# Three of sixteen low halves from GpSimd to VectorE, and the gates' copy at the head of its chunk

## The chip, the core and the metric

One core of a Trainium2 chip runs the whole program. It has TensorE (matmuls into PSUM), VectorE, ScalarE, GpSimd (which works on SBUF here) and the DMA queues; each runs its own instruction stream, and they wait for one another on semaphores. The metric is device time in microseconds, lower is better. Of the kernel before, three runs took 857.78, 859.27 and 860.64 us; the median is 859.27.

## The reference

4096 tokens of 128 features go through two blocks with residuals.

```python
x = x + gnn(layernorm(x), adj, ...)       # two-head masked attention over 4096 tokens
# then the block that the change touches; xf = layernorm(x), 4096 x 128:
gate_scores = xf @ Wg + bg                # 8 experts
mask = one_hot(top_k(gate_scores, 2)).sum(-2)
h = gelu(einsum('td,edh->teh', xf, W1) + b1)    # all 8 experts, 256 hidden
y = einsum('teh,ehd->ted', h, W2) + b2
out = x + einsum('ted,te->td', y, mask)   # the two chosen experts, weight 1 each
```

## The kernel before

The attention takes the first three quarters of the time, tile by tile of 128 rows. The change touches only the feed-forward block behind it, which runs from about 657 us to the end.

The tokens stand in 8 chunks j of 512 (`NC`, `CH`). Each chunk computes all 8 experts e densely, and a 0/1 gate per token and expert picks two of them at the end. The precision of float32 comes from pairs of float16: a value is kept as a high half (rounded to f16) and a low half (the rest), and each product is three matmuls: high by high, high by low, low by high.

For an expert the hidden layer comes in two blocks b of 128 (`HB` is 2), so a chunk has 16 hidden blocks of 128x512, numbered 2e+b. The path of one is:

- TensorE, `up` (L986 to L988): three 128x512 matmuls into one of 4 PSUM banks. It waits for the Gelu that empties the bank.
- ScalarE, `ffn` (L468): Gelu from PSUM to `hid`, f32. Then (L471) a copy to `hid_hi`, f16.
- GpSimd, `ffn` (L337): `hid - hid_hi` to `hid_lo`, f16, all of them in the order of 2e+b. `hid`, `hid_hi` and `hid_lo` lie in the buffer `prob`, so the profile calls all three that. They have 8 slots, four experts.
- TensorE, `down` (L1006 to L1008): 24 matmuls of 128x128 into a PSUM bank of two, for both blocks of e. It waits for both low halves (`hid_lo_ready`, L995) and for the combination of expert e-2 (`combined`), which empties the bank.
- VectorE, `combine` (L772): four 128x128 operations, `x_sb = psum * gate + x_sb`.

TensorE's order is written out in `ffn`: in step e it does up(e), then down(e-2), the latter two steps of the next chunk for e of 6 and 7. So down(j, 0) runs in step 2 of the chunk, and the last two of a chunk in steps 0 and 1 of the next.

Beside the experts runs the second bias, which depends on the gate. VectorE copies the gates of the chunk, 128x32, to f16 (`halve_gates`, L753). TensorE transposes them in step 3, between up(3) and down(1) (`gate_transpose`, L965, four operations). ScalarE copies the result (L458), TensorE multiplies it with the bias in step 4 (L974, L975), and VectorE adds that to `x_sb` behind the combination of e=2 (`add_b2`, L760).

VectorE's order in a chunk is: combine 0, halve_gates, combine 1, combine 2, add_b2, combine 3 to 7. In the first chunk (`early`) it also finishes the last two tiles of the attention: normalise (L654) behind combine 0, and behind combine 5 the ranking of the last four tiles' gates (`rank_gates`, L680 to L687, seven of them at L687, 128x4 each) and behind combine 6 their choice (`choose_gates`, L693 to L695). All these read and write SBUF. Every engine does its stream strictly in the written order.

Of the kernel before, what the change touches and what calls it, by code (L numbers as in the profile page):

```python
# [9 lines left out]
ALU = mybir.AluOpType  # L10
# [15 lines left out]
E, H, HB = 8, 256, 2  # L26
# [21 lines left out]
UP_BANKS = 4  # L48
HID_RING = 8
DOWN_LAG = 2  # L50


def build(nc, x, adj, wq, wk, wv, wr, wd, bias, wg, bg, w1, b1, w2, b2, out):
# [6 lines left out]
    with ExitStack() as ctx:  # L60
# [3 lines left out]
        def sem(name):  # L64
            return ctx.enter_context(nc.semaphore(name))
# [58 lines left out]
        hid = prob[:, 1, :].rearrange("p (r c) -> p r c", r=HID_RING)  # L124
        hid_hi = area(0, 0, NC // 2).bitcast(F16).rearrange("p (r c) -> p r c", r=HID_RING)
        hid_lo = area(0, NC // 2, NC // 2).bitcast(F16).rearrange("p (r c) -> p r c", r=HID_RING)
# [69 lines left out]
        hid_raw_ready = sem("hid_raw_ready")  # L196
        hid_hi_ready = sem("hid_hi_ready")
        hid_lo_ready = sem("hid_lo_ready")
        down_done = sem("down_done")
        combined = sem("combined")  # L200

# [10 lines left out]
        def copies_by_dve(j, units):  # L212

            return NU // 2 * j + units // 2

        block = ctx.enter_context(nc.Block())
        N_QKV_W, N_W = 3, 8
# [49 lines left out]
        @block.gpsimd  # L267
        def _(pool):
            pool.memset(ident[:, :], 0.0).then_inc(ident_zero, 1)
            pool.wait_ge(ident_zero, 1)  # L270
            pool.affine_select(out=ident[:, :], in_=ident[:, :], compare_op=ALU.not_equal, fill=1.0, base=0,
                               pattern=[[-1, P]], channel_multiplier=1).then_inc(ident_ready, 1)
            pool.memset(wrd[:, :, :, :], 0.0).then_inc(wrd_zero, 1)
            pool.memset(expo[:, :], -0.5).then_inc(ones_ready, 1)

            def load_adj(i, par):

                for c in range(2):
                    if not isinstance(i, int) or i >= 2:
                        pool.wait_ge(masked, NU * i - 12 + 4 * c)  # L280
                    cols = slice(c * HALF, (c + 1) * HALF)
                    pool.dma_start(mask[:, par, cols], adj[bass.ds(i * P, P), cols],  # L282
                                   max_dma_last_dim=8192).then_inc(adj_in[par][c], 16)

            def inverse_std_x(i):

                part = slice(i * X_TILES, (i + 1) * X_TILES)
                pool.wait_ge(var_ready, i + 1)
                pool.tensor_tensor(rstd[:, part], ve[:, part], expo[:, part], ALU.pow).then_inc(rstd_ready, 1)

            def split_weights(n, raw, pair):

                pool.tensor_scalar(raw, raw, W_UP, 0.0, ALU.mult, ALU.add).then_inc(w_split_chain, 1)
                pool.wait_ge(w_split_chain, 3 * n + 1)
                pool.tensor_scalar(pair[:, 0, :], raw, 1.0, 0.0, ALU.mult, ALU.add).then_inc(w_split_chain, 1)
                pool.wait_ge(w_split_chain, 3 * n + 2)
                pool.tensor_tensor(pair[:, 1, :], raw, pair[:, 0, :], ALU.subtract).then_inc(w_split_chain, 1)

            pool.wait_ge(ones_ready, 1)
            for i in range(X_PARTS):  # L300
                inverse_std_x(i)
            load_adj(0, 0)
            load_adj(1, 1)
            pool.wait_ge(k_lo_ready, NC)
            pool.wait_ge(w1_in, 16)
            split_weights(0, w1_raw, w1_pair)
            pool.wait_ge(w2_in, 16)
            split_weights(1, w2_raw, w2_pair)
            pool.wait_ge(w_in, 16 * N_W)
            split_weights(2, wg_sb[:, :], wg_pair)  # L310
            split_weights(3, b2_sb[:, :], b2_pair)
            pool.tensor_scalar(ident16[:, :], ident[:, :], 1.0, 0.0, ALU.mult, ALU.add).then_inc(w_split_chain, 1)

            def inverse_std(t0):

                pool.wait_ge(ve2_ready, t0 + PAIR)
                pool.tensor_tensor(rstd2[:, :], ve2[:, :], expo[:, 0:PAIR], ALU.pow).then_inc(rstd2_ready, PAIR)

            def load_behind_post(i, par):

                if par == 0:
                    inverse_std(i - 6)
                load_adj(i, par)

            for i in range(2, 6):
                load_adj(i, i % 2)
            pairs(pool, 6, NT, load_behind_post)
            for t0 in range(NT - 6, NT, PAIR):
                inverse_std(t0)

            def ffn(j, par):
                for e in range(E):
                    for b in range(HB):

                        slot = (2 * e + b) % HID_RING
                        pool.wait_ge(hid_hi_ready, 16 * j + 2 * e + b + 1)  # L336
                        pool.tensor_tensor(hid_lo[:, slot, :], hid[:, slot, :], hid_hi[:, slot, :],  # L337
                                           ALU.subtract).then_inc(hid_lo_ready, 1)

            pairs(pool, 0, NC, ffn)  # L340
# [141 lines left out]
        def _(dve):  # L482
# [265 lines left out]
            def halve_gates(j):  # L748

                if not isinstance(j, int) or j > 0:  # L750
                    dve.wait_ge(gatet_psum, j)
                settled()
                dve.tensor_copy(gate16, gate[:, bass.ds(j * TPC, TPC), :]).then_inc(gate16_ready, 1)  # L753

            def add_b2(j):
# [4 lines left out]
                dve.tensor_tensor(x_sb[:, rows, :], ps[:, PREP0, :].rearrange("p (t d) -> p t d", d=D), x_sb[:, rows, :],  # L760
                                  ALU.add).then_inc(acc_ready, 1)

            def combine(j, e):

                dve.wait_ge(down_done, 8 * j + e + 1)
                if e == 3:
                    dve.wait_ge(acc_ready, j + 1)
                elif e > 0:
                    dve.wait_ge(combined, 8 * j + e)
                for t in range(TPC):  # L770
                    row = x_sb[:, bass.ds(j * TPC + t, 1), :].rearrange("p t d -> p (t d)")
                    ins = dve.scalar_tensor_tensor(row, ps[:, DOWN0 + e % 2, t * D:(t + 1) * D],  # L772
                                                   gate[:, bass.ds(j * TPC + t, 1), e:e + 1].rearrange("p t e -> p (t e)"),
                                                   row, ALU.mult, ALU.add)
                ins.then_inc(combined, 1)

            def ffn(j, par, early=False):

                for e in range(E):
                    combine(j, e)  # L780
                    if e == 0:
                        halve_gates(j)
                    if e == 2:
                        add_b2(j)
                    if early and e == 0:
                        normalise(NT - PAIR)
                    if early and e == 3:
                        x2t_low(NT - PAIR, bank=PREP0 + 1)
                    if early and e == 5:
                        keep_logits(NT - PAIR, bank=PREP0 + 1)  # L790
                        rank_gates(1, RANKED_EARLY, NT)
                    if early and e == 6:
                        choose_gates(1, RANKED_EARLY, NT)
# [6 lines left out]
        def _(pe):  # L800
# [189 lines left out]

            def down(j, e, early=False):

                pe.wait_ge(hid_lo_ready, 16 * j + 2 * e + 2)
                if not (early and e < 2):
                    pe.wait_ge(combined, 8 * j + e - 1)  # L995
                elif e == 0:
                    pe.wait_ge(sat_ready, NT)
                else:
                    pe.wait_ge(logit_ready, NT - PAIR)
                for t in range(TPC):  # L1000
                    bank = ps[:, DOWN0 + e % 2, t * D:(t + 1) * D]
                    for b in range(HB):
                        slot = (2 * e + b) % HID_RING
                        rows = slice(t * P, (t + 1) * P)
                        cols = slice((HB * e + b) * D, (HB * e + b + 1) * D)
                        pe.matmul(bank, hid_hi[:, slot, rows], w2_pair[:, 0, cols], start=(b == 0), stop=False)  # L1006
                        pe.matmul(bank, hid_hi[:, slot, rows], w2_pair[:, 1, cols], start=False, stop=False)  # L1007
                        ins = pe.matmul(bank, hid_lo[:, slot, rows], w2_pair[:, 0, cols], start=False, stop=(b == HB - 1))  # L1008
                ins.then_inc(down_done, 1)

            def ffn(j, par, early=False):

                for e in range(E):
# [9 lines left out]
                    if e == 4:  # L1023
                        gates_b2(j)
                    if e >= DOWN_LAG:
                        down(j, e - DOWN_LAG, early)
                    elif not early:
                        down(j - 1, e + E - DOWN_LAG)

# [26 lines left out]
```

## Time and profile before

| | |
|---|---|
| runs shown, median | 859.27 us (857.78 to 860.64) |
| the profiled execution's own time | 858.09 us |
| its span | 856.1 us |
| TensorE matmuls busy | 812.1 us, 95% |
| TensorE weight loads | 596.3 us, 70% |
| ScalarE | 678.9 us, 79% |
| VectorE | 624.6 us, 73% |
| GpSimd | 221.3 us, 26% |

The profile page gives for each engine the busy time, and for each group of instructions the count, the mean duration and the idle time ahead of them with what ended it. Matmuls overlap: a 128x512 one shows 0.38 us but the next starts earlier, so distances between starts tell the rate, not durations. GpSimd's share of 26% is an average; in the feed-forward block its busy tenths are 7 or 8, those of TensorE 9, of VectorE 3 or 4. TensorE's granted clock is full (1.00, which is 2.4 GHz) in that block but for a stretch of some 6 us near its start at half of it, behind a pause of TensorE.

### The profile page before, as it was taken

The numbers are of one execution on the slowest core, as the hardware profiler recorded it, in microseconds if no ns is written. First come the engines' busy times: TensorE is split into PE (matmuls) and PEld (weight loads), VectorE is DVE, ScalarE is ACT, GpSimd is POOL, SyncE is SP. The second block draws the span as 40 slices with busy tenths as digits, with TensorE's granted clock in tenths as the row PEclk, the third lists the DMA queues.
The fourth block names the chain that finished last, engine by engine and source line by source line (L and its number), as shares of the span: only waits on it lengthen the run. The fifth ranks groups of instructions, "written<-read, shape, count | busy, mean of one in ns | idle before, by whom it ended". The sixth has DMA issues, their size and how long they took to land.

```text
span 856.1 us, 31746 instructions
## 1 busy us (share of the span) xinstructions
PE 812.1 (95%) x12080; PEld 596.3 (70%) x12080; DVE 624.6 (73%) x1506; ACT 678.9 (79%) x1099; POOL 221.3 (26%) x233
## 2 busy tenths in 40 slices
PE   4969999999999999999999999999987889999997
PEld 1627777777777777777777777777765656666675
DVE  6587888888888888888888888888883374444444
ACT  3838887878788787887878788787877678998985
POOL 4180000100100000010000001000000778878785
PEclk9989999999999999999999999999999899999999
DMA  8515533443343344334334433433100000000000
GB/s 219 108 22 91 82 58 58 66 75 55 58 77 55 55 70 71 55 60 75 55 55 74 67 55 62 73 55 57 29 0 2 2 14 14 14 13 12 12 12 12
DMA packets 40900, 44.96 MB, mean 53 GB/s; under 512 B 22168, under 2 KB 32160, under 8 KB 40864
## 3 DMA queue, kind: packets, MB, share of 16 engines
q0 software_dynamic: 9216, 33.56, 24.7%
q1 hardware_dynamic: 31216, 10.71, 5.4%
q8 instruction: 24, 0.39, 0.2%
q10 hardware_dynamic: 432, 0.20, 0.1%
q14 instruction: 12, 0.10, 0.0%
HBM read 71.72 MB, written 2.10 MB: 86 GB/s over the span
## 4 chain that ended last, share of the span: by engine, by line
PE 72%; POOL 17%; issue 6%; DVE 3%; DMA 1%; POOLq 1%; DVEq 0%; ACT 0%
PE ps L892 28%; PE ps L861 19%; PE ps L876 19%; POOL prob L337 17%; PE ps L903 2%; DVE prob L577 1%; PE ps L817 1%; PE ps L822 1%; PE ps L830 1%; PE ps L911 1%; PE ps L808 1%; DMA x_sb<-in_x 1%; POOLq L336 0%; DVE stats L501 0%; DVE mask L545 0%
## 5 line engine op out<-in xcount | busy, mean ns | idle before, releaser
L577 DVE CUSTOM_DVE_ANT_0 prob<-ps,mask 128x1024 f32<-128x1024 f32 x256 | 312.0, 1220 | 90.4 <-PE ps L861 84.6
L406 ACT ACTIVATE prob<-prob,nmax 128x1024 f32<-128x1024 f32 x256 | 292.8, 1144 | 9.9 <-DVE nmax L585 9.9
L892 PE MATMUL ps<-pt,v_sb 128*64 128x128 f32 x4096 | 251.6, 276 | 0.0
L892 PEld LDWEIGHTS ps<-pt,v_sb 128*64 128x64 f32 x4096 | 221.0, 137 | 13.4 <-issue 7.5
L421 ACT ACTIVATE pt<-ps 128x1024 f32<-128x1024 f32 x128 | 131.1, 1024 | 112.6 <-PE ps L876 112.6
L876 PEld LDWEIGHTS ps<-ident,prob 64*128 64x128 f32 x4096 | 151.9, 139 | 79.4 <-issue 79.3
L861 PE MATMUL ps<-k_half,q_row 64*128 64x512 f16 x1536 | 190.0, 380 | 4.8 <-DVE low L577 4.8
L876 PE MATMUL ps<-ident,prob 64*128 64x64 f32 x4096 | 182.9, 228 | 10.3 <-DVE pt L595 5.7
L337 POOL TENSOR_TENSOR prob<-prob 128x512 f16<-128x512 f32 x128 | 148.2, 1160 | 38.5 <-ACT prob L471 33.6
L282 POOL DMA_DIRECT2D mask<-in_adj x64 | 35.5, 554 | 429.4 <-DVE low L577 429.4
L772 DVE SCALAR_TENSOR_TENSOR x_sb<-ps,k_half,x_sb 128x128 f32 (+1 forms) x256 | 72.1, 344 | 99.5 <-PE ps L1008 99.2
L861 PEld LDWEIGHTS ps<-k_half,q_row 64*128 64x128 f16 x1536 | 71.5, 96 | 68.4 <-issue 9.6
L468 ACT ACTIVATE prob<-ps,b_sb 128x512 f32<-128x512 f32 x128 | 86.9, 679 | 25.4 <-PE ps L988 23.6
L1006 PE MATMUL ps<-w_pair,prob 128*128 128x128 f16 x512 | 90.3, 221 | 6.6 <-POOL prob L337 4.7
L595 DVE COPY pt<-ps 128x512 f32<-128x512 f32 x128 | 88.1, 688 | 9.7 <-PE ps L876 8.7
L1008 PE MATMUL ps<-w_pair,prob 128*128 128x128 f16 x512 | 90.1, 220 | 0.0
L1007 PE MATMUL ps<-w_pair,prob 128*128 128x128 f16 x512 | 90.1, 220 | 0.0
L471 ACT ACTIVATE prob<-prob 128x512 f16<-128x512 f32 x128 | 80.7, 630 | 4.1
L418 ACT ACTIVATE pt<-ps 128x512 f32<-128x512 f32 x128 | 75.1, 587 | 1.1 <-PE ps L876 1.1
L1006 PEld LDWEIGHTS ps<-w_pair,prob 128*128 128x128 f16 x512 | 50.4, 98 | 14.6 <-POOL prob L337 5.4
L1007 PEld LDWEIGHTS ps<-w_pair,prob 128*128 128x128 f16 x512 | 50.5, 99 | 5.1
L1008 PEld LDWEIGHTS ps<-w_pair,prob 128*128 128x128 f16 x512 | 50.5, 99 | 0.0
(96 smaller groups left out, 657.7 us busy)
## 6 DMA issues: line engine op xcount, KB each, us to landing
mask<-in_adj POOLq DMA_DIRECT2D x64, 512.0 KB, 5.6
q_row<-q_nat SPq DMA_DIRECT2D x128, 32.0 KB, 4.8
x_sb<-in_x SPq DMA_DIRECT2D x4, 512.0 KB, 7.0
out<-x_sb SPq DMA_DIRECT2D x8, 256.0 KB, 2.3
pt<-in_L_ffn_W SPq DMA_DIRECT2D x1, 1024.0 KB, 6.5
wq_sb<-in_L_gnn_Wq ACTq DMA_DIRECT2D x1, 64.0 KB, 2.9
wk_sb<-in_L_gnn_Wk ACTq DMA_DIRECT2D x1, 64.0 KB, 4.5
wv_sb<-in_L_gnn_Wv ACTq DMA_DIRECT2D x1, 64.0 KB, 5.6
```

The costliest lines, as they stand in the source:

```text
L337: pool.tensor_tensor(hid_lo[:, slot, :], hid[:, slot, :], hid_hi[:, slot, :], ALU.subtract).then_inc(hid_lo_ready, 1)
L406: act.activation(prob[:, h, cols], prob[:, h, cols], ACT.Exp, bias=nmax[:, h:h + 1], scale=-1.0, accum_out=sums[:, j, h, p:p + 1]).then_in ...
L421: act.activation(pt[:, u, :, :].rearrange("p k (b q) -> p b k q", b=2), ps[:, TR0:TR0 + 2, :].rearrange("p b (k q) -> p b k q", k=KT), ACT ...
L468: act.activation(hid[:, slot, :], ps[:, (2 * e + b) % UP_BANKS, :], ACT.Gelu, bias=b1_sb[:, e, b:b + 1], scale=1.0 / W_UP).then_inc(hid_ra ...
L577: dve.tensor_tensor_reduce(out=prob[:, h, col_of(p)], in0=ps[:, 2 * (u % 2):2 * (u % 2) + 2, :].rearrange("p b c -> p (b c)"), in1=mask[:, ...
L595: dve.tensor_copy(pt[:, u, :, DH:P], ps[:, TR0 + 1, :].rearrange("p (k q) -> p k q", k=KT)).then_inc(pt_by_dve, 1)
L861: ins = pe.matmul(ps[:, 2 * (u % 2) + half, :], q_row[part, par, h, a, :], k_half[part, h, b, cols], start=first, stop=final)
L876: ins = pe.transpose(ps[:, TR0 + half, t * DH:(t + 1) * DH], prob[part, h, (p * KT + t) * P:(p * KT + t + 1) * P], ident[part, part])
L892: ins = pe.matmul(ps[dims, AV, 0:P], v_sb[:, tile, dims], pt[:, UNITS.index((h, p)), t, :], start=(tile == 0), stop=(tile == NT - 1))
L1006: pe.matmul(bank, hid_hi[:, slot, rows], w2_pair[:, 0, cols], start=(b == 0), stop=False)
L1007: pe.matmul(bank, hid_hi[:, slot, rows], w2_pair[:, 1, cols], start=False, stop=False)
L1008: ins = pe.matmul(bank, hid_lo[:, slot, rows], w2_pair[:, 0, cols], start=False, stop=(b == HB - 1))
```

## The change

A constant names three experts, e = 2, 4 and 6. Their second hidden block (b = 1) gets its low half from VectorE (`low_hidden`), not from GpSimd; that is three of the sixteen of a chunk, 24 in all. GpSimd's loop leaves it out. VectorE does the one of expert e+1 just ahead of the combination of e, so behind the combination of e-1, and for e+1 = 4 behind `add_b2` as well. It counts on a semaphore of its own, and `down` waits for both counts. The gates' copy moves from behind combine 0 to the head of the chunk, ahead of combine 0.

```diff
+DVE_LOWS = (2, 4, 6)
+        hid_lo_by_dve = sem("hid_lo_by_dve")
+        POOL_LOWS = HB * E - len(DVE_LOWS)
+
+        def lows_by_dve(j, e):
+
+            return len(DVE_LOWS) * j + sum(1 for d in DVE_LOWS if d <= e)
+
+        def lows_by_pool(j, e):
+
+            return POOL_LOWS * j + HB * (e + 1) - sum(1 for d in DVE_LOWS if d <= e)
@@ GpSimd
                 for e in range(E):
-                    for b in range(HB):
+                    for b in range(1 if e in DVE_LOWS else HB):
@@ VectorE
+            def low_hidden(j, e):
+
+                slot = (2 * e + 1) % HID_RING
+                dve.wait_ge(hid_hi_ready, 16 * j + 2 * e + 2)
+                dve.tensor_tensor(hid_lo[:, slot, :], hid[:, slot, :], hid_hi[:, slot, :],
+                                  ALU.subtract).then_inc(hid_lo_by_dve, 1)
@@ VectorE, ffn
+                halve_gates(j)
                 for e in range(E):
+                    if e + 1 in DVE_LOWS:
+                        low_hidden(j, e + 1)
                     combine(j, e)
-                    if e == 0:
-                        halve_gates(j)
                     if e == 2:
                         add_b2(j)
@@ TensorE, down
-                pe.wait_ge(hid_lo_ready, 16 * j + 2 * e + 2)
+                pe.wait_ge(hid_lo_ready, lows_by_pool(j, e))
+                pe.wait_ge(hid_lo_by_dve, lows_by_dve(j, e))
```

## Rows read from the trace of the kernel before

**Rows 1.** Waits of TensorE, last stage: engine, line, releaser: us, times, longest.

```profile
PE ps L965 <- DVE k_half L753: 5.4, 7, 0.9
PE ps L1006 <- POOL prob L337: 4.7, 2, 4.0
PE ps L1006 <- DVE x_sb L772: 1.9, 1, 1.9
```

**Rows 2.** Busy time (instructions) by engine in one stretch, then granted clock, DMA share, GB/s.

```profile
760.00:780.00 20.00, 19.25 (x223) 13.78 (x221) 8.82 (x30) 17.83 (x29) 15.98 (x14) 1.00 0.04 13
```

**Rows 3.** TensorE's timeline in one chunk: start us, us, engine, line, operation [idle before <-releaser].

```profile
765.35 0.38 PE L988 MATMUL ps<-x2t_hi,w_pair 128*128 x1
766.48 0.39 PE L965 MATMUL ps<-ident,k_half 128*8 128x128 f16 x4 [0.75 <-DVE k_half L753]
766.79 0.23 PE L1006 MATMUL ps<-w_pair,prob 128*128 128x128 f16 x1
775.15 0.38 PE L988 MATMUL ps<-x2t_hi,w_pair 128*128 x1
775.36 0.22 PE L1006 MATMUL ps<-w_pair,prob 128*128 128x128 f16 x1
778.00 0.22 PE L1006 MATMUL ps<-w_pair,prob 128*128 128x128 f16 x1
```

**Rows 4.** VectorE's timeline in the same chunk and the start of the next.

```profile
764.71 1.13 DVE L772 SCALAR_TENSOR_TENSOR x_sb<-ps,k_half,x_sb 128x128 f32 x4 [1.64 <-PE ps L1008]
765.75 0.67 DVE L753 CAST k_half<-k_half 128x32 f16 x1
771.74 1.13 DVE L772 SCALAR_TENSOR_TENSOR x_sb<-ps,k_half,x_sb 128x128 f32 x4 [2.16 <-PE ps L1008]
772.97 0.69 DVE L760 TENSOR_TENSOR x_sb<-ps,x_sb 128x512 f32 x1
774.38 1.12 DVE L772 SCALAR_TENSOR_TENSOR x_sb<-ps,k_half,x_sb 128x128 f32 x4 [0.71 <-PE ps L1008]
784.92 1.13 DVE L772 SCALAR_TENSOR_TENSOR x_sb<-ps,k_half,x_sb 128x128 f32 x4 [1.51 <-PE ps L1008]
788.73 0.67 DVE L753 CAST k_half<-k_half 128x32 f16 x1
```

**Rows 5.** Timelines of VectorE and TensorE around the start of the second chunk.

```profile
694.19 1.02 DVE L695 TENSOR_SCALAR k_half<-k_half 128x32 f32<-128x32 f32 x1
695.25 2.16 DVE L772 SCALAR_TENSOR_TENSOR x_sb<-ps,k_half,x_sb 128x128 f32<-128x128 f32 x8
697.33 0.17 DVE L753 CAST k_half<-k_half 128x32 f16<-128x32 f32 x1
697.55 0.39 PE L965 MATMUL ps<-ident,k_half 128*8 128x128 f16 x4 [0.93 <-DVE k_half L753]
```

**Rows 6.** Line L687 in the last stage: operation, count, duration min/median/max ns, starts.

```profile
L687 DVE TENSOR_TENSOR k_half<-k_half x7: 167/987/1145, 687.7 to 691.5; 128x4 f32<-128x4 f32 x7
```

**Rows 7.** ScalarE's timeline behind the gate transposes of that chunk.

```profile
767.62 0.57 ACT L458 ACTIVATE k_half<-ps 8x512 f16<-8x512 f16 x1
769.07 0.69 ACT L468 ACTIVATE prob<-ps,b_sb 128x512 f32<-128x512 f32 x1 [0.89 <-PE ps L988]
```

**Rows 8.** Groups by shape, whole span: out<-in, count, busy us, mean ns, idle before.

```profile
L538 DVE TENSOR_TENSOR k_half<-ps,k_half 128x512 f16<-128x512 f32 x8 | 5.3, 687 | 1.8 <-ACT k_half L374 1.8
L628 DVE SCALAR_TENSOR_TENSOR o_act<-o_pre 128x256 f32<-128x256 f32 x16 | 6.7, 416 | 0.0
L337 POOL TENSOR_TENSOR prob<-prob 128x512 f16<-128x512 f32 x128 | 148.2, 1160 | 38.5 <-ACT prob L471 33.6
```

**Rows 9.** GpSimd's timeline at the sixth expert (e=5) of that chunk.

```profile
773.79 2.40 POOL L337 TENSOR_TENSOR prob<-prob 128x512 f16<-128x512 f32 x2 [0.89 <-ACT prob L471]
```

**Rows 10.** Line L995, a wait ahead of the second layer, on TensorE's queue: durations in ns.

```profile
L995 PEldq ALU_OP  x33: 32/32/32, 712.5 to 845.1; - x33
L995 PEldq EVENT_SEMAPHORE  x20: 51/51/51, 673.2 to 849.8; - x20
```

## The prediction

> **What bounds the kernel now.** I read the waits of TensorE first, over the last stage only, because the change touches nothing ahead of it. Beyond its start, that stage has two kinds of wait [rows 1]: 5.4 us in 7 pieces at L965, the gate transposes, until VectorE's copy of the gates (L753), and 1.9 us once at L1006 until a combination. The 4.7 us until GpSimd are 4.0 us before the very first second-layer matmul and 0.7 us before the last expert's; neither falls at an expert whose low half moves. Then the table by stretches [rows 2]: TensorE is busy 19.25 of 20 us at clock 1.00, GpSimd 15.98, VectorE 8.82. So TensorE sets the pace and GpSimd is nowhere late within a chunk. The chain of waits walks along GpSimd's L337 for 17% of the span, which is misleading: with its pieces stands "issue", and no matmul in the steady part waits for it.
>
> Then TensorE's own timeline in one chunk [rows 3]. In a run of matmuls without a wait a 128x512 one starts 0.216 us after the one before (775.15, then 775.36), although its modelled duration is 0.38. The last one of the first layer's fourth expert (e=3) starts at 765.35, so TensorE could go on at 765.57; the transposes start at 766.48. The loss is 0.91 us, 0.16 more than the 0.75 the row names (0.38 less 0.22, the modelled tail). The expert period without a stall is 778.00 - 775.36 = 2.64 us. VectorE's timeline [rows 4] shows the cause: the combination of e=0 starts at 764.71 and ends at 765.84, the copy follows at 765.75 and takes 0.67 us to 766.42, and 0.06 us later TensorE starts. The same copy takes 0.17 us at 697.33 [rows 5], where GpSimd had nothing to do.
>
> **The change, part by part.**
>
> *The copy moves ahead of all combinations of the chunk.* It now stands right behind the previous chunk's last combination, the one at 784.92, which ends at 786.05. Beside GpSimd the copy takes 0.67 us, and the longest that any such small two-port operation took is 1.145 us (L687, [rows 6]), so it is done by 787.2 at worst. The period is 788.73 - 765.75 = 22.98 us, so the next transposes could start at 765.57 + 22.98 = 788.55: 1.3 us to spare. The semaphore it waits for, the previous chunk's transposes, fired some 19 us earlier. What is late next: TensorE goes straight from up(3) to the transposes and down(1), then up(4), whose first Gelu would be ready at 769.07 - 0.91 = 768.16, while ScalarE's copy of the transposed gates ends at 767.62 + 0.57 = 768.19 [rows 7]: ScalarE is just in time. Over a chunk it is busy 17.83 / 20 x 22.98 = 20.5 us [rows 2], so at a period of 22.1 it is still not the bound. So the whole stall goes. Sum over the stage: 5.4 + 7 x 0.16 = 6.5 us. (In the second chunk the piece is 0.93 + 0.16 = 1.09 us: the transposes at 697.55 could have started at 696.46 [rows 5]. There the copy would follow the combination that starts at 695.25 and ends at 696.3, so it is done at 696.5 even if nothing before it gets shorter; and L695, which took 1.02 us at 694.19 beside GpSimd's second low half of e=2, gets shorter as that one goes.) In the first chunk there is no stall and TensorE waits neither way.
>
> *Three low halves move to VectorE.* GpSimd's takes 1.16 us [rows 8]. Nobody waits for these, so taking 24 of 128 away from GpSimd (28 us of busy time) is worth nothing by itself. On VectorE: 128x512 with f16 out is 0.687 us with one operand in PSUM (L538), and 128x256 with both in SBUF 0.416 us (L628); 256 more elements at VectorE's rate in these two rows make the second about 0.69 us too. Bounds 0.69 alone and 0.69 + 1.15 behind GpSimd's operation; never below 0.69. Do they fit? e=2: behind the combination of e=0, from 765.75 to 766.44; down(2) starts more than an expert period behind down(1) at 766.79 [rows 3], so after 769.4, 3 us to spare. e=6: in the 1.51 us of idle time that a combination in the even run has ahead of it [rows 4]; down(6) comes 5.3 us behind down(4), and it fits alike. e=4 is the tight one: combination of e=2 from 771.74, the second-layer bias at 772.97 to 773.66, then the low half, then the combination of e=3 at 774.38 [rows 4]. Operations without a wait of their own start about 0.09 us before the recorded end of the last (765.75 against 765.84), so 773.57 to 774.26. That is before 774.38, and 1.1 us ahead of down(4) at 775.36. GpSimd's next, the first half of e=5, wants to start at 773.79 [rows 9], 0.22 us behind VectorE. If the two exclude each other GpSimd is held until 774.26, ends its pair at about 776.7, and down(5) is at 778.00. All of these shift together by the 0.91 us, so the order holds afterwards. I take nothing for this part, with the loss of that race as a rival.
>
> The rows show the exclusion: seven operations of 4 elements (L687) took up to 1.145 us where 0.167 is their least, all beside GpSimd's back-to-back low halves. The Trainium skill (SBUF — State Buffer, Who interferes with whom) says that a VectorE operation with two SBUF inputs and a GpSimd operation that reads SBUF exclude each other for a whole instruction, and that the issue order decides who is blocked. That speaks against this change, whose added operations are of that kind. By it the sum stays 5.2 us if VectorE is first and becomes rival A's if GpSimd is; without any exclusion it stays 5.2 us.
>
> *A second semaphore wait ahead of each second-layer group on TensorE.* Its queue handles such a wait in 0.051 us, with 0.032 us for the arithmetic ahead of it [rows 10]: 0.083 us. With the present two waits, down(1) starts 0.31 us after the first of four transposes, 0.08 us more than four steps of 0.056 (an expert period less six of 0.216, through 24). A third would make 0.14 into 0.22 from matmul to matmul. Behind a 128x512 matmul 0.216 us cover that; behind the short ones of the gates (down(1) and down(2) of each chunk) it is exposed. Bounds: 0, and 64 x 0.083 = 5.3 us. I take 16 x 0.083 = 1.3 us, since at 775.15 to 775.36 nothing of the two waits shows.
>
> *Ends.* The chunk order at the very end is the same: e=7 stays with GpSimd. The first 4.0 us stall stays. The first chunk's copy now comes before its first combination, beside the short GpSimd operation that the stall begins with: between 0 and the copy's own 0.17 us [rows 5], and I take 0.
>
> Sum: -6.5 + 1.3 = **-5.2 us**. The profiled execution took 858.09 us (span 856.1 and 2.0 around it), so it would be 852.9; the median of the runs shown is 1.2 us higher, 859.27, and from it comes **854.0**.
>
> **Rivals.**
>
> A. GpSimd wins the race at e=4. VectorE's low half then waits for 773.79 + 1.16 = 774.95, ends at 775.64, and down(4) starts 0.06 us later instead of at 775.36: 0.33 us per chunk, 2.7 us in all; result -2.5 us, 856.7. For: only 0.22 us between the two, worked out from an overlap of another pair. Against: both hang on the same TensorE stretch, so the gap doesn't wander.
>
> B. VectorE is starved of the shared access at e=4: it gets in only behind both halves of e=5, at 776.19, and ends at 776.88. down(4) is 1.58 us late in each chunk, 12.6 us; -5.2 + 12.6 = +7.4, 866.7, slower. It decides from a delay of 0.65 us per chunk, that is when the low half ends behind 775.95. For: GpSimd leaves only 0.08 us between its two. Against: the seven L687, of which none waited longer than one operation.
>
> C. The third wait is exposed at every group: 5.3 us against 6.5, so -1.2, 858.1, no change. For: TensorE's queue must pass two instructions per 0.056 us in the second layer, little reserve. Against: 0.21 us of cover, and rows with no sign of two waits.
>
> D. The transposes are still late, for another releaser (the copy blocked, or ScalarE at e=4 later than I reckon): half of the 6.5 stays, -2.0, 857.3, within the noise.
>
> **How the numbers follow.** Forecast 0.70, A 0.12, C 0.09, D 0.04, B 0.05. What can be told from no change is 0.3%, 2.6 us. A lies on that bound, 0.07 of it count as faster and 0.05 as same. Faster 0.77, same 0.05 + 0.09 + 0.04 = 0.18, slower 0.05. The range: below, the wait costs nothing and the run lies with the profiled one: 859.27 - 6.5 - 1.2 = 851.6. Above, it takes in A and most of D: 857.3. Left out are C and B, 0.14, and a little of the rest.
>
> **What would show it.** Right: no wait at L965 for L753; transposes 0.22 us behind the last matmul of up(3); chunk period about 22.1 to 22.2 us instead of 22.98; L753 right behind the last combination; new VectorE operations of about 0.69 us, the one of e=4 ahead of GpSimd's; clock 1.00 throughout. Wrong: L1006 waiting for VectorE's low half at e=4 (A, B: 0.3 or 1.6 us), gaps ahead of every L1006 with no releaser (C), L965 waiting still (D).

## The result and the profile after

The changed kernel took 851.53 us (median of 4 runs, 851.02 to 852.68); the kernel before took 858.52 beside it (4 runs, 857.45 to 860.64). The ratio is 0.9919, 95% interval 0.9903 to 0.9935, so 7.0 us (5.6 to 8.3) less. I had forecast 854.0, 5.2 us less, in a range from 851.6. The direction and the place were right. The size was not, and the time lies 0.07 us below the range. Two later comparisons of the same kernel, on different chips, gave 0.9929 (0.9911 to 0.9947) and 0.9938 (0.9924 to 0.9952), 6.1 and 5.3 us less. Microseconds beside a ratio are worked out from it, here and below.

The waits of TensorE in the feed-forward block of the kernel after, from the view of waits (the line numbers are new: L1027 is the first matmul of the second layer, L985 the gate transposes):

```profile
PE ps L1027 <- POOL prob L349: 4.7, 2, 4.0
PE ps L1027 <- DVE x_sb L791: 1.9, 1, 1.9
```

Of the three kinds in [rows 1] the one at the transposes is gone; the two others are as they were, to the tenth. The same stretch as in [rows 2] now has TensorE busy in all 20 us, and GpSimd 2.5 us less:

```profile
760.00:780.00 20.00, 20.00 (x234) 14.45 (x232) 10.93 (x33) 18.60 (x30) 13.48 (x12) 1.00 0.05 13
```

TensorE's timeline after, at the place of [rows 3]: the last matmul of up(3), the transposes, down(1).

```profile
762.03 0.38 PE L1008 MATMUL ps<-x2t_hi,w_pair 128*128 x1
762.34 0.39 PE L985 MATMUL ps<-ident,k_half 128*8 128x128 f16 x4
762.66 0.23 PE L1027 MATMUL ps<-w_pair,prob 128*128 128x128 f16 x1
```

From 762.03 to 762.34 it is 0.31 us, where it was 1.13 [rows 3]. That is 0.82 us per chunk, not the 0.91 that I reckoned with. From transposes to down(1) it is 0.32 us with three waits, and was 0.31 with two (starts are printed to 0.01 us; copy_alone below has two waits and 0.32 us).

Parts of VectorE's timeline after, from the last combination of one chunk on (L765 is the gates' copy, L779 the new low halves):

```profile
758.62 1.12 DVE L791 SCALAR_TENSOR_TENSOR x_sb<-ps,k_half,x_sb 128x128 f32 x4 [1.51 <-PE ps L1029]
759.71 0.76 DVE L765 CAST k_half<-k_half 128x32 f16 x1
761.26 1.24 DVE L791 SCALAR_TENSOR_TENSOR x_sb<-ps,k_half,x_sb 128x128 f32 x4 [0.79 <-PE ps L1029]
762.42 0.68 DVE L779 TENSOR_TENSOR prob<-prob 128x512 f16<-128x512 f32 x1
768.84 0.69 DVE L772 TENSOR_TENSOR x_sb<-ps,x_sb 128x512 f32 x1
769.45 0.68 DVE L779 TENSOR_TENSOR prob<-prob 128x512 f16<-128x512 f32 x1
770.24 1.12 DVE L791 SCALAR_TENSOR_TENSOR x_sb<-ps,k_half,x_sb 128x128 f32 x4
```

The copy ends at 760.47, 1.9 us ahead of the transposes. It still takes 0.76 us, since GpSimd is at work beside it, but nobody waits for it there. The low half of e=4 starts at 769.45, 0.08 us before the recorded end of the bias, as forecast. GpSimd's first half of e=5 follows 0.20 us later and is the one that is held:

```profile
769.65 1.50 POOL L349 TENSOR_TENSOR prob<-prob 128x512 f16<-128x512 f32 x1 [2.12 <-ACT prob L483]
```

It takes 1.50 us where 1.16 is usual. All 24 low halves on VectorE took nearly the same time, so in none of the chunks was VectorE the one to wait; this is the line over the whole kernel after, with minimum, median and maximum in ns:

```profile
L779 DVE TENSOR_TENSOR prob<-prob x24: 677/682/689, 670.4 to 840.4; 128x512 f16<-128x512 f32 x24
```

Where the time went, from the starts of single matmuls in TensorE's timelines. "Start" is the first matmul of the feed-forward block, "gates" the first gate transpose of a chunk.

| us | before | after |
|---|---|---|
| start | 656.98 | 657.48 |
| start to gates of the first chunk | 14.63 | 13.57 |
| to gates of the second | 25.94 | 24.82 |
| six further chunks | 137.84 | 132.94 |
| to the end | 20.71 | 20.69 |
| span | 856.1 | 849.5 |

The rows give +0.50, -1.06, -1.12, -4.90 and -0.02, in sum -6.6. The way between gates accounts for 1.12 + 4.90 = 6.0, of which 5.9 are the stall: in the second chunk the transposes came 1.31 us behind the last matmul of up(3), and now come 0.31 us behind it, so 1.00 of the 1.12 is stall (the rest is the end of the half-clock stretch, which before reached past the first gates). What remains are +0.50 in the attention, which the change doesn't touch, and -1.06 ahead of the first gates, where TensorE had no such stall. There the two traces differ in the clock. These are stretches of 1 us (TensorE's busy time and its number of matmuls, then the granted clock, the DMA share and GB/s) of the kernel before:

```profile
665.00:666.00 1.00, 0.05 (x1) 0.55 0.00 0
666.00:667.00 1.00, 1.00 (x11) 0.50 0.06 16
670.00:671.00 1.00, 1.00 (x3) 0.50 0.00 0
671.00:672.00 1.00, 1.00 (x7) 0.54 0.00 0
```

and of the kernel after:

```profile
666.00:667.00 1.00, 0.56 (x9) 0.93 0.00 0
667.00:668.00 1.00, 1.00 (x13) 0.50 0.08 16
670.00:671.00 1.00, 1.00 (x6) 0.86 0.00 0
671.00:672.00 1.00, 1.00 (x18) 1.00 0.00 0
```

In both, TensorE stood idle for 4.0 us before that, and the clock went from 2.4 to 1.2 GHz. Before, it had fallen while TensorE was still idle and was low from 665.1 to 671.9, 6.8 us; after, it fell when TensorE was at work again and was low from 666.9 to 670.3, 3.4 us (a slice of mean clock m was low for 2(1 - m) of its length). These replace the "some 6 us" of the section on the profile before and the 6.3 and 3.6 us of the expectations below.

### The profile page after: what moved, and what is told of

It reads as the page before. It is cut to its first block, busy times and chain, and to the rows that moved or that the text cites. A ratio compares the mean times of both kernels' runs of the same rounds, so it can differ in the third digit from the quotient of the medians.

```text
span 849.5 us, 31821 instructions
## 1 busy us (share of the span) xinstructions
PE 811.7 (96%) x12080; PEld 597.7 (70%) x12080; DVE 639.2 (75%) x1530; ACT 679.0 (80%) x1099; POOL 195.5 (23%) x209
## 4 chain that ended last, share of the span: by engine, by line
PE 73%; POOL 14%; issue 8%; DVE 3%; DMA 1%; ACT 0%; POOLq 0%; DVEq 0%
PE ps L912 28%; PE ps L881 19%; PE ps L896 19%; POOL prob L349 14%; PE ps L923 2%; PE ps L837 1%; PE ps L842 1%; PE ps L850 1%; DVE prob L589 1%; PE ps L931 1%; PE ps L828 1%; DMA x_sb<-in_x 1%; DVE stats L513 0%; POOLq L348 0%; ACT prob L418 0%
## 5 line engine op out<-in xcount | busy, mean ns | idle before, releaser
L349 POOL TENSOR_TENSOR prob<-prob 128x512 f16<-128x512 f32 x104 | 122.6, 1183 | 57.1 <-ACT prob L483 54.4
L1027 PE MATMUL ps<-w_pair,prob 128*128 128x128 f16 x512 | 89.9, 220 | 6.6 <-POOL prob L349 4.7
L1029 PE MATMUL ps<-w_pair,prob 128*128 128x128 f16 x512 | 89.8, 220 | 0.0
L1027 PEld LDWEIGHTS ps<-w_pair,prob 128*128 128x128 f16 x512 | 50.3, 98 | 14.6 <-POOL prob L349 5.4
L1029 PEld LDWEIGHTS ps<-w_pair,prob 128*128 128x128 f16 x512 | 50.4, 98 | 0.0
```

## The experiments

Theory: the gain is the stall at the gate transposes, which needs only that the copy is ready in time. Rivals: GpSimd's relief carries part of it; the stretch at half clock belongs to the change; the waits on TensorE's queue cost something. "Block" below is the span of the profiled execution less the start of the feed-forward block; it leaves out the attention, whose length went from 656.98 to 659.67 us from one profiled execution to another, though only the last two kernels below touch it.

**The changed kernel again** (whole_again; no edit).

> The changed kernel once more, beside the others on one chip. Theory S (the gain is the stall at the gate transposes: 0.82 us less in each of chunks 3 to 8, 1.1 in the second, 6.0 in all): -6.0 us against the kernel before. Theory C (a further 1.06 us come from a shorter stretch at half clock in the first chunk, and belong to the change): -7.0 us, and the stretch at half clock is again about 3.5 us long. If C is chance, its length varies from run to run as in the kernel before.

0.9929 (0.9911 to 0.9947), -6.1 us. Block 192.0 us, as after (849.5 - 657.48 = 192.0); before 199.1. The half-clock stretch was 3.4 us, as in the first profile of the changed kernel. This alone did not tell S from C.

**The copy alone** (copy_alone, against the kernel before).

```diff
+                halve_gates(j)
                 for e in range(E):
                     combine(j, e)
-                    if e == 0:
-                        halve_gates(j)
```

> Only the gates' copy moves to the head of the chunk; GpSimd keeps all sixteen low halves, one wait on TensorE less than in the changed kernel. Theory S: the same as the changed kernel, -6.0 us, chunk period 22.15 us, L965 without a wait. Rival R (the relief of GpSimd carries part of the gain, because the copy behind two GpSimd operations would still be late or the shorter L695 counts): at least 1 us less gain, -5 or less.

0.9927 (0.9908 to 0.9946), -6.3 us. TensorE doesn't wait at the transposes and the period between gates is 22.16 us, that of the changed kernel. Within the noise of the runs the whole gain of the change is in this half of it, and R at its 1 us is out.

The profile shows a small part of R. The block is 192.6 us, 0.5 more than the changed kernel's, and all of that lies ahead of the first gates: 14.12 us from the start instead of 13.57, with the same 3.4 us at half clock. TensorE waits 0.31 us there for the normalised last two tiles (view of waits), because VectorE's normalisation runs beside GpSimd's unbroken row of six low halves. The row of copy_alone, then that of the kernel after, where GpSimd's row has five and ends before:

```profile
670.62 1.59 DVE L654 TENSOR_SCALAR x<-x_sb,mv,rstd 128x128 f32<-128x128 f32 x2
```

```profile
669.91 0.60 DVE L666 TENSOR_SCALAR x<-x_sb,mv,rstd 128x128 f32<-128x128 f32 x2
```

So the low halves add 0.5 us, once. The ratios of the two kernels (0.9927 and 0.9929) can't show it.

**The low halves alone** (lows_alone, against the changed kernel).

```diff
-                halve_gates(j)
                 for e in range(E):
                     if e + 1 in DVE_LOWS:
                         low_hidden(j, e + 1)
                     combine(j, e)
+                    if e == 0:
+                        halve_gates(j)
```

> Only the three low halves move; the gates' copy stays behind the first combination. Theory S with exclusion between VectorE and GpSimd: the copy no longer meets GpSimd's second half of e=2, so it takes 0.17 instead of 0.67 us and the stall falls from 0.82 to 0.32 us per chunk: period 22.48 us, -3.2 us in all. If the low halves did nothing at all for the copy (no exclusion): 0 us. If the moved low halves are a cost: slower.

0.9938 (0.9921 to 0.9955), -5.3 us, more than the 3.2 expected. The mechanism is as expected. VectorE's timeline of this kernel, combination of e=0, copy, low half of e=2:

```profile
764.27 1.13 DVE L791 SCALAR_TENSOR_TENSOR x_sb<-ps,k_half,x_sb 128x128 f32 x4 [1.64 <-PE ps L1030]
765.31 0.17 DVE L765 CAST k_half<-k_half 128x32 f16 x1
765.39 0.69 DVE L779 TENSOR_TENSOR prob<-prob 128x512 f16<-128x512 f32 x1
```

The copy takes 0.17 us instead of 0.67 [rows 4], because GpSimd's second half of e=2 is no longer beside it, and the waits show what is left:

```profile
PE ps L986 <- DVE k_half L765: 1.5, 6, 0.3
```

The period is 22.48 us, 0.50 less than before, as written down. I had left two things out of that sum, and both are seen against the second profile of the kernel before (before_again below), which has the same 3.4 us at half clock: the second chunk gives 0.84 us more (24.97 against 25.81), and the way to the first gates 0.78 (13.55 against 14.33), where GpSimd's shorter row lets the normalisation through. With the six periods, 2.95, that is -4.6 by the trace, well inside the interval of the ratio (-6.8 to -3.9). So the halves of the change overlap: at the transposes each removes the same stall, one all of it and the other 0.5 us of it per chunk. They don't add, and that the low halves came along is worth about 0.5 us in the first chunk, and nothing behind it, once the copy has moved.

**Four more waits on TensorE** (four_waits, against the changed kernel).

```diff
                 pe.wait_ge(hid_lo_by_dve, lows_by_dve(j, e))
+                for _ in range(4):
+                    pe.wait_ge(hid_hi_ready, 16 * j + 2 * e + 2)
```

> The changed kernel with four more semaphore waits, always met already, ahead of each of the 64 second-layer groups (7 instead of 3). What I predicted of a wait (0.083 us each where no long matmul covers it, 0.216 us of cover behind a first-layer matmul): 0.083 x 4 x 16 = 5.3 us for those behind the short gate matmuls and (0.14 + 0.42 - 0.216) x 48 = 16 us for the others, 21 us slower than the changed kernel. Rival: TensorE's queue runs ahead of its array, so waits already met cost nothing: within 1 us of the changed kernel.

0.9920 (0.9902 to 0.9938), -6.9 us, block 192.2 us. The term of my prediction is refuted at the place for which I had reckoned it. TensorE's timeline with seven waits ahead of L1029, at the transposes:

```profile
764.30 0.38 PE L1008 MATMUL ps<-x2t_hi,w_pair 128*128 x1
764.61 0.39 PE L985 MATMUL ps<-ident,k_half 128*8 128x128 f16 x4
764.93 0.23 PE L1029 MATMUL ps<-w_pair,prob 128*128 128x128 f16 x1
```

Each of the added waits that the trace holds (140 of 256) does take its 51 ns on the queue:

```profile
L1016 PEldq EVENT_SEMAPHORE  x140: 51/51/51, 663.1 to 845.0; - x140
```

but the distance from transposes to down(1) is 0.32 us with seven as with three. The queue is ahead of the array there by more than these 0.2 us.

At one place of the whole block it isn't. In the first chunk TensorE waits 0.25 us for VectorE, does six matmuls that start 0.03 us apart, and then comes a second-layer group:

```profile
682.46 0.18 PE L940 MATMUL ps<-wg_pair,x2t_hi 128*128 128x8 f16 x1 [0.25 <-DVE x2t_lo L674]
682.60 0.17 PE L942 MATMUL ps<-wg_pair,x2t_lo 128*128 128x8 f16 x1
682.79 0.22 PE L1029 MATMUL ps<-w_pair,prob 128*128 128x128 f16 x1
```

The last distance is 0.19 us; in whole_again, with three waits, it is 0.02 (682.70 to 682.72). So met waits can cost: right behind a real wait, where the queue had nothing in hand, four of them cost 0.17 us, once.

**The kernel before again** (before_again; no edit).

> The kernel before once more, for the part of the profiled gain that the stall doesn't explain: from the first matmul of the feed-forward block to the first gate transposes the profiled execution of before took 14.63 us with 6.3 us at half clock, the changed kernel 13.57 with 3.6. Theory V (the moment at which the clock falls is chance; the part is no part of the change): this profile shows a stretch near 3.5 us and about 13.6 us for that part, or another value again. Theory P (it belongs to the kernel before): 6.3 and 14.6 us again. Time: no change.

0.9993 (0.9982 to 1.0004). Start 658.05, first gates at 672.38: 14.33 us, and the half-clock stretch was 3.4 us, not 6.8:

```profile
667.00:668.00 1.00, 0.99 (x15) 0.84 0.00 0
668.00:669.00 1.00, 1.00 (x13) 0.50 0.07 16
671.00:672.00 1.00, 0.48 (x2) 0.96 0.00 0
```

Those 14.33 us hold 0.5 us of a wait for the last two tiles' normalised input:

```profile
PE ps L911 <- DVE x L654: 0.5, 1, 0.5
```

copy_alone has 0.3 us of it, the changed kernel none, and neither has the first profile of before, whose longer stretch at half clock had TensorE late itself. The length of the low stretch is not the kernel's.

**The changed kernel a third time** (whole_third; no edit).

> The changed kernel beside early_six on one chip, and a fourth profile of the stretch at half clock: about 3.5 us again if 6.3 us in the first profile of before was chance. Against the kernel before -6.0 to -7.0 us.

0.9938 (0.9924 to 0.9952), -5.3 us, less than the 6.0 to 7.0 expected. Here the changed kernel had the long stretch, low from the pause until 672.1, and 14.62 us from start to first gates, as the first profile of before:

```profile
665.00:666.00 1.00, 0.00 (x0) 0.64 0.00 0
666.00:667.00 1.00, 0.88 (x9) 0.50 0.00 0
672.00:673.00 1.00, 1.00 (x18) 0.94 0.00 0
```

So V holds: both kernels show both lengths. But the 1.06 us were not all luck of one pair of profiled executions. Like against like, from start to first gates:

| us | before | after |
|---|---|---|
| 3.4 us at half clock | 14.33 | 13.57 |
| 6.8 us at half clock | 14.63 | 14.62 |

There is one profile of the kernel before in each row. With the short stretch 0.76 us belong to the change (by copy_alone 0.2 of it to the copy's move and 0.55 to the low halves), with the long one nothing. The block is 6.6 us shorter in the first case (198.7 against 192.0) and 5.9 in the second (199.1 against 193.2).

**The low halves late** (lows_late, against the changed kernel).

```diff
-                    if e + 1 in DVE_LOWS:
-                        low_hidden(j, e + 1)
                     combine(j, e)
+                    if e + 1 in DVE_LOWS:
+                        low_hidden(j, e + 1)
```

> The changed kernel with each of VectorE's low halves behind the combination of e instead of ahead of it, so that it comes when GpSimd is busy with its own pair, and is late for TensorE. It measures what my rivals A and B lived on. With exclusion (VectorE waits until GpSimd's running operation ends): the low half takes up to 1.4 us instead of 0.68, and down of e=2, 4, 6 is late by 0.4, 1.6 and 1.6 us: 28 us slower than the changed kernel. Without: 0.68 us each, 0.2, 0.8 and 0.8 us late, 14 us slower.

1.0219 (1.0197 to 1.0241), 18.8 us slower than before; its span is 25.8 us longer than the changed kernel's. That fits exclusion (28) and not its absence (14). The low halves in this kernel, and one of them beside GpSimd's pair of e=5:

```profile
L779 DVE TENSOR_TENSOR prob<-prob x24: 683/1304/1343, 674.1 to 865.6; 128x512 f16<-128x512 f32 x24
```

```profile
780.63 2.39 POOL L349 TENSOR_TENSOR prob<-prob 128x512 f16<-128x512 f32 x2 [2.48 <-ACT prob L483]
```

```profile
782.27 1.31 DVE L779 TENSOR_TENSOR prob<-prob 128x512 f16<-128x512 f32 x1
```

VectorE's operation starts at 782.27 and ends at 783.58, 0.56 us behind GpSimd's end at 783.02. The one that comes second is held, whichever it is. TensorE waited for it:

```profile
PE ps L1027 <- DVE prob L779: 17.6, 18, 1.3
```

For GpSimd it waited 9.1 us instead of 4.7. This is the price of having all three low halves late. What the race at e=4 alone costs, which the change wins by 0.20 us, the next kernel shows.

**Six low halves** (six_lows: `DVE_LOWS = (1, 2, 3, 4, 5, 6)`).

> The changed kernel with one low half each of e=1 to 6 on VectorE (48 instead of 24). Theory (GpSimd's relief is worth nothing in the even run): the chunk period stays 22.15 us. Where VectorE ranks the last gates, GpSimd's operation at the last of the seven small ones (L699) goes, 1.0 us: the wait for the combination, 1.9 us, becomes 0.9, -1.0 us in all. Rival (VectorE becomes late with six): a wait of TensorE for VectorE's low halves in every chunk, slower.

0.9914 (0.9893 to 0.9936), -7.4 us against before; block 191.6 us, 0.5 less than the changed kernel's. The wait for the combination behind the ranking fell:

```profile
PE ps L1027 <- DVE x_sb L791: 1.1, 1, 1.1
```

by 0.8, a little less than reckoned. The view of waits names none for VectorE's low halves, but two periods were 22.27 and 22.43 us instead of 22.16, and there the other 0.4 us stayed. The second is the race at e=4, lost once in the eight chunks; GpSimd, VectorE and down(4):

```profile
746.74 1.16 POOL L349 TENSOR_TENSOR prob<-prob 128x512 f16<-128x512 f32 x1 [2.13 <-ACT prob L483]
746.77 1.68 DVE L779 TENSOR_TENSOR prob<-prob 128x512 f16<-128x512 f32 x1
748.58 0.23 PE L1027 MATMUL ps<-w_pair,prob 128*128 128x128 f16 x1
```

GpSimd starts 0.03 us ahead, VectorE's low half takes 1.68 us and ends at 748.45, and down(4) starts 0.25 us later than in the changed kernel. early_six lost it at the same place. The first is at down(1) of the second chunk, which starts 0.10 us behind the end of the low half of e=1 (695.35) and 0.13 later than usual; that it waited for it is my reading.

**An earlier start** (early_start, against the changed kernel).

```diff
-            for t0 in range(NT - 6, NT, PAIR):
+            for t0 in range(NT - 6, NT - PAIR, PAIR):
                 inverse_std(t0)
@@ GpSimd, first chunk only
+                    if early and e == 2:
+                        inverse_std(NT - PAIR)
@@ TensorE, first chunk only: behind down(1) instead of ahead of the gate transposes
+                    if early and e == 3:
+                        x2_transpose(NT - PAIR, bank=PREP0 + 1)
```

> The changed kernel, but GpSimd does the low halves of the first two experts of the first chunk before it computes the last two tiles' inverse deviation (it waited for VectorE's statistics in front of them), and TensorE transposes those tiles behind down(1) of the first chunk instead of ahead of the gates. Theory: the 4.0 us wait ahead of the very first second-layer group goes, and with it the stretch at half clock (3.6 us, so 1.8 us of loss): from first matmul to first gate transposes 7.7 instead of 13.57 us, -5.9 us against the changed kernel, -12 us against the kernel before, near 846. Rival: the wait moves on, to the transposes of the last two tiles or to ScalarE's copy of them, and more than 2 us of it stay.

0.9871 (0.9847 to 0.9894), 848.20 us, by the ratio 11.1 less than the kernel before. From start to first gates 7.68 us (expected 7.7), and the clock is 1.00 throughout; the 4.0 us wait is gone, 0.7 of 4.7 is left at the end:

```profile
PE ps L1031 <- DVE x_sb L795: 1.9, 1, 1.9
PE ps L1031 <- POOL prob L351: 0.7, 1, 0.7
PE ps L935 <- DVE x L670: 0.4, 1, 0.4
```

Of 5.9 us, 5.1 reach the end (block 187.0): the way to the second chunk's gates is 25.64 us instead of 24.82, in part by the new 0.4 us at L935.

**Both** (early_six).

> early_start and six_lows together. Their gains lie at different places (the first second-layer group, 5.8 us; the ranking of the last gates, 0.8 us less of a wait), so they should add: feed-forward block 192.0 - 5.1 - 0.5 = 186.4 us from its first matmul to the end, 5.6 to 6.5 us below the changed kernel. If they don't add, because the earlier start meets the ranking elsewhere: as early_start.

0.9873 (0.9857 to 0.9888), 847.60 us, and block 187.8: no better than early_start. The ranking's wait is 1.1 us, but the wait for the last two tiles is 1.3 us at L935, where early_start has 0.4:

```profile
PE ps L935 <- DVE x L670: 1.3, 1, 1.3
PE ps L1031 <- DVE x_sb L795: 1.1, 1, 1.1
```

The gains did not add; the low half of e=1 stands ahead of the first combination and of the normalisation behind it, and the normalisation then takes 1.92 us beside two of GpSimd's operations, where it takes 1.27 in early_start.

## Why the prediction was right or wrong

**The stall goes: right, and 0.6 us too large.** "So the whole stall goes. Sum over the stage: 5.4 + 7 x 0.16 = 6.5 us": no wait at L985, in the changed kernel and in copy_alone. The measured sum is 5.9 (1.00 + 4.90). I took the spacing of long matmuls, 0.216 us, for the distance at which the transposes could follow; from the second chunk on it is 0.31 without any wait, in every kernel here that has none. So 0.1 us of each 0.91 could never go.

**The copy in time: right.** Ready 1.9 us ahead; held by GpSimd (0.76 us) at no cost. ScalarE was just in time and not the bound: its share is 18.60 of 20 us, with TensorE busy all the time.

**The three low halves worth nothing: right in the even run where it is added to the copy's move, wrong in the first chunk, incomplete by itself.** From the second chunk on the sum's zero holds (copy_alone's period is the whole's). "In the first chunk there is no stall and TensorE waits neither way" does not: a term that I put at nothing measures 0.76 us in the profiles with the short stretch at half clock, 0.5 of it by the low halves, and nothing in those with the long one. And I had seen the copy at 0.17 us where GpSimd had nothing to do [rows 5] and did not draw the conclusion that taking away GpSimd's second half of e=2 would shorten it in every chunk. lows_alone shows 0.50 us per chunk.

**The race at e=4: right.** VectorE came first in all chunks, at the place and with the 0.2 us that the prediction had worked out. Rival A would have been an exclusion against VectorE, and lows_late shows that it exists: 1.31 instead of 0.68 us. Where the race was lost, once in six_lows, it cost 0.25 us; the prediction had reckoned 0.33 per chunk. The Trainium skill's rule (SBUF — State Buffer, Who interferes with whom), that two SBUF inputs on VectorE and a reading GpSimd operation exclude each other and that the order of issue decides, agrees with both traces: GpSimd is held at 769.65 in the changed kernel, VectorE at 782.27 in lows_late. Whether VectorE could be starved (rival B) was not tried.

**The third wait: the step that failed.** "I take 16 x 0.083 = 1.3 us" was a term of the wrong size; it measures 0, in the changed kernel (0.32 us against 0.31) and with four waits more (0.32 us again; 0.17 us in all, at another place). I had added the wait's duration on its queue to the distance between matmuls; that 0.08 us appear ahead of down(1) with two waits doesn't mean that the waits make them, and with seven they are the same 0.08. Rival C falls with it.

**The range.** -6.5 + 1.3 = -5.2 should have been -5.9 + 0, and up to 0.8 us more in the first chunk. From 859.27 the -5.9 make 853.4; and the median of before was 0.75 us lower by the time of comparison, 858.52, which gives 852.6, or 851.9 with the first chunk. What is left to 851.53 lies within the interval of the ratio, and the repeats (-6.1 and -5.3 us) lie on both sides of -5.9. The low end of my range had room for a third wait that costs nothing, but not for the first chunk's gain. And it left no room for the long and the short stretch at half clock, which moves an execution by about 1 us, nor for the length of the attention, which moves it by 2.7.

## What to carry to other kernels

A small copy on a path that the busiest engine waits for belongs ahead of the work that doesn't need it; what it cost here was mostly its place in the order, and partly GpSimd's operation beside it, so look for both before splitting the work anew. A duration on a queue is no cost until it shows between two operations of TensorE's array: compare the distance at a place with the distance at another place of the same kind that has no wait. When two edits remove the same stall they don't add, so try each alone. A view of waits can leave out short ones: the lost race of six_lows stands in no line of it and shows only in the starts of single matmuls. And compare profiled executions only with those in which the clock did the same.

## What the runs showed of the hardware

- A group with an 8-row or 8-column weight operand starts 0.31 us behind a 128x512 matmul instead of 0.216, and the 128x128 group behind it starts 0.15 us behind its last matmul where 0.056 is usual, whatever the number of waits (2, 3 or 7). The cause stays open; the profile puts the idle time of the weight loads ahead of it down to "issue".
- After the same 4.0 us pause, TensorE ran at 1.2 GHz for 3.4 us in eight profiled executions and for 6.8 us in two, one of the kernel before and one of the changed one. In the long ones the clock had already fallen within the pause (0.8 us before its end), in the short ones 0.3 to 1.2 us after TensorE had resumed. Without the pause (early_start) it stayed at 2.4 GHz there.
- If VectorE's subtraction (0.68 us) starts first, GpSimd's takes 1.50 us instead of 1.16 when it comes 0.20 us later. If its own 1.16 us are unchanged it was held for 0.34 us, so by this estimate VectorE lets go about 0.54 us after its start, 0.14 us before its recorded end.
- Four waits more on TensorE's queue, 51 ns each, cost nothing where matmuls were running before them, and 0.17 us right behind a real wait and six short matmuls (four_waits).
- VectorE's normalisation of two 128x128 tiles takes 0.59 to 0.60 us by itself and 1.59 us beside GpSimd's unbroken row of low halves (copy_alone).
